# Attention A: the transfers of the relative-position rows split once more, into even and odd rows

## The reference

```python
pos   = (sinusoid_pos_emb(S, D) @ Wp + bp)          # S x 16 per head
content_score = einsum('bhsp,bhtp->bhst', q + u, k)
pos_score     = einsum('bhsp,htp->bhst',  q + v, pos)
pos_score     = _relative_shift(pos_score)
weights = softmax((content_score + pos_score) / sqrt(16))
out     = weights @ val

def _relative_shift(x):                              # b, h, s, s
    x = pad(x, one zero column in front)             # rows of s+1
    x = x.reshape(b, h, s + 1, s)                    # read again as rows of s
    return x[:, :, 1:, :].reshape(b, h, s, s)
```

## Time and profile before

| what | us |
|---|---|
| median of three runs | 11101.68 (11082.91 to 11107.82) |
| the profiled execution, its own time | 11115.23 |
| its span, first to last instruction | 11113.4 |
| busy: TensorE / ScalarE / VectorE / GpSimd | 9422.7 / 6687.5 / 6258.0 / 2944.3 |
| transfers in attention A, writes and reads | 2048 + 2048, 512 KB each |

### The profile page before, as it was taken

The page is one execution under the profiler, slowest core; times in us unless marked ns, Lnnn a source line. Parts: engine busy times, 40 slices in busy tenths (PEclk is TensorE's granted clock), DMA queues, the critical chain, the costliest instruction groups (busy, mean ns, idle before and its releaser), DMA issues. The chain is left out here.

```text
span 11113.4 us, 271423 instructions
## 1 busy us (share of the span) xinstructions
PE 9422.7 (85%) x95520; PEld 6711.5 (60%) x95520; DVE 6258.0 (56%) x14730; ACT 6687.5 (60%) x11009; POOL 2944.3 (26%) x3520
## 2 busy tenths in 40 slices
PE   5888888999688888899968888889996888888999
PEld 3665665666465666566646656656663565665666
DVE  3655663765365566376446556637644565663764
ACT  3666663765466666376546666637644666663764
POOL 2333332001233333200123333310012333331001
PEclk7999999999899999999989999999998999999999
DMA  6999992000699999100069999911007999991100
GB/s 240 378 363 366 381 378 87 26 25 16 233 377 366 361 379 380 59 25 25 16 254 380 367 362 382 365 46 27 23 18 265 373 372 362 379 357 48 27 22 26
DMA packets 747623, 2482.45 MB, mean 223 GB/s; under 512 B 111745, under 2 KB 133761, under 8 KB 745921
## 3 DMA queue, kind: packets, MB, share of 16 engines
q1 hardware_dynamic: 746176, 2463.84, 60.3%
HBM read 1280.34 MB, written 1183.07 MB: 222 GB/s over the span
## 5 line engine op out<-in xcount | busy, mean ns | idle before, releaser
L658 DVE CUSTOM_DVE_ANT_0 z<-sc,z 128x1024 f32<-128x1024 f32 x2048 | 2496.5, 1220 | 1848.5 <-DMA z<-rel_rows 1608.0
L716 POOL TENSOR_SCALAR z<-z,nmax 128x1024 f32<-128x1024 f32 x2048 | 2277.8, 1123 | 4028.5 <-DVE nmax L668 4028.5
L631 ACT ACTIVATE pT<-rg 128x512 f32<-128x512 f32 x4096 | 2445.9, 598 | 738.7 <-PE rg L541 679.5
L541 PE MATMUL rg<-ident,z 128*128 128x128 f32 x16384 | 2527.0, 277 | 77.0 <-issue 68.3
L639 ACT ACTIVATE rel<-rg 128x512 f32<-128x512 f32 x3072 | 1721.1, 596 | 1407.2 <-PE rg L522 1401.8
L541 PEld LDWEIGHTS rg<-ident,z 128*128 128x128 f32 x16384 | 1990.3, 142 | 784.6 <-ACT rel L639 294.4
L522 PE MATMUL rg<-pos_s,qv_s 96*128 96x512 bf16 x4096 | 1590.8, 396 | 1021.4 <-DVE rel L693 901.6
L1013 DVE CUSTOM_DVE_ANT_0 z<-sc,mask 128x1024 f32<-128x1024 f32 (+7 forms) x1536 | 1359.1, 910 | 227.0 <-PE sc L832 173.9
L952 ACT ACTIVATE pT<-rg 128x512 f32<-128x512 f32 (+3 forms) x1792 | 928.4, 550 | 763.0 <-PE rg L885 751.0
L522 PEld LDWEIGHTS rg<-pos_s,qv_s 96*128 96x128 bf16 x4096 | 478.7, 118 | 1498.0 <-DVE rel L693 1150.9
L960 ACT ACTIVATE z<-z,nmax 128x128 f32<-128x128 f32 (+15 forms) x1024 | 1226.6, 1198 | 89.0 <-POOL nmax L978 76.7
(11 more groups left out here) (93 smaller groups left out, 8161.5 us busy)
## 6 DMA issues: line engine op xcount, KB each, us to landing
rel_rows<-rel SPq DMA_DIRECT2D x2048, 512.0 KB, 7.2
z<-rel_rows SPq DMA_DIRECT2D x2048, 512.0 KB, 7.1
xnT<-qu_parts SPq DMA_DIRECT2D x792, 64.0 KB, 2.3
xnT<-v_heads SPq DMA_DIRECT2D x132, 256.0 KB, 4.3
v_heads<-rel SPq DMA_DIRECT2D x8, 4096.0 KB, 12.5
k_sb<-k_parts SPq DMA_DIRECT2D x408, 64.0 KB, 2.3
qv_s<-qv_parts SPq DMA_DIRECT2D x384, 64.0 KB, 6.2
pos_s<-pos_parts SPq DMA_DIRECT2D x384, 64.0 KB, 7.2
```

What stands on the lines that cost most here:

```text
L541: mm = e.transpose(rg[:, T_BANK[q], (j - 4 * q) * P:(j - 4 * q + 1) * P], z[:, n % RING, j * P:(j + 1) * P], ident[:, :])
L631: e.activation(pT[:, t % 2, q * CH:(q + 1) * CH], rg[:, T_BANK[q], :], ACT.Exp, scale=SCALE).then_inc(p_ready[q], 1)
L658: e.tensor_tensor_reduce(out=zs, in0=scf[:, 2 * half * CH:2 * (half + 1) * CH], in1=zs, scale=1.0, scalar=-3.0e38, op0=ALU.add, op1=ALU.ma ...
L716: e.tensor_scalar(zs, zs, 1.0, nmax[:, n % 2:n % 2 + 1], ALU.mult, ALU.add).then_inc(AA[done], 1)
```

## The change

Each column half of a write or a read becomes two transfers of 64 rows x 1024 floats, one of the even and one of the odd rows: 64 partitions in steps of 2 on the SBUF side, a row pitch of two rows in device memory. Within a half the order is read even, write even, read odd, write odd. The write's waits stand ahead of the even write only. The counts of the two semaphores go from 32 to 64 a tile.

```diff
-                                for per in (G, G // OB, 32 * G // RING, HB // NB * QK_INC, HB // NB * 16)))
+                                for per in (G, G // OB, 64 * G // RING, HB // NB * QK_INC, HB // NB * 16)))
...
-            return base.moves + 32 * (n // RING + 1)
+            return base.moves + 64 * (n // RING + 1)
...
-            def read_half(n, half):
+            def read_part(n, half, odd):
...
-                shifted = bass.AP(tensor=rel_d.tensor, offset=hd * FLAT + (i0 + 1) * S + c0, ap=[[S, P], [1, S // 2]])
-                e.dma_start(z[:, k, c0:c0 + S // 2], shifted).then_inc(rel_in[k], 16)
-
-            def write_half(base, n, half):
+                shifted = bass.AP(tensor=rel_d.tensor, offset=hd * FLAT + (i0 + odd + 1) * S + c0,
+                                  ap=[[2 * S, P // 2], [1, S // 2]])
+                e.dma_start(z[odd:P:2, k, c0:c0 + S // 2], shifted).then_inc(rel_in[k], 16)
+
+            def write_part(base, n, half, odd):
...
-                for c in ((R_DVE, R_ACT[-1]) if half else (R_ACT[1],)):
-                    e.wait_ge(r_copied[c], e.snap(base.tiles + (n + 1)))
-                    settle(e)
-                there = bass.AP(tensor=rel_d.tensor, offset=hd * FLAT + i0 * (S + 1) + 1 + c0, ap=[[S + 1, P], [1, S // 2]])
-                e.dma_start(there, rel[:, k, c0:c0 + S // 2]).then_inc(rel_out[k], 16)
+                if not odd:
+                    for c in ((R_DVE, R_ACT[-1]) if half else (R_ACT[1],)):
+                        e.wait_ge(r_copied[c], e.snap(base.tiles + (n + 1)))
+                        settle(e)
+                there = bass.AP(tensor=rel_d.tensor, offset=hd * FLAT + (i0 + odd) * (S + 1) + 1 + c0,
+                                ap=[[2 * (S + 1), P // 2], [1, S // 2]])
+                e.dma_start(there, rel[odd:P:2, k, c0:c0 + S // 2]).then_inc(rel_out[k], 16)
...
                 for half in range(2):
-                    if here(n):
-                        read_half(n, half)
-                    if here(r):
-                        write_half(base, r, half)
+                    for odd in range(2):
+                        if here(n):
+                            read_part(n, half, odd)
+                        if here(r):
+                            write_part(base, r, half, odd)
```

## The result

The changed kernel takes **12165.01 us** (median of 4 runs, 12142.59 to 12186.07) against 11104.75 us before: a ratio of 1.0958, 95% interval 1.0927 to 1.0989. It is slower by 1060 us; I had said 11830, and 11040 to 12500 as the range. The profile after has a span of 12142.9 us, 1029.5 more than before.

The account below looks back on a forecast made before the run. Attention A, 55% of the span, was taken to last as long as its DMA packets take. 11115 us plus 690 for stepped rows and 41 for small packets made 11846, less 14 for the median: some 11830, range 11040 to 12500.

Parts of the forecast that it names:

- What bounds the kernel: Attention A, 55% of the span, lasts as long as its DMA packets take; the queue is always full.
- Bytes, finer alternation: Attention A's transfers: bytes and large packets stay, finer turns between reads and writes save nothing; taken as 0, at best -563 us.
- Small packets: Four more transfers a tile add 64 small packets at 10 ns each, 4 on each engine: 41 us.
- Stepped rows: Attention A's transfers of 64 rows in steps of two have slower packets: +690 us, at most +2072; chance 0.45.
- rival 1: The queue hides all: stepping costs nothing, only small packets are left; 11102 to 11160 us, chance 0.22.
- SP's queue: SP's four more issues a step, 1.3 to 1.9 us, are covered by its 2.1 us of waiting: 0.
- rival 2: SP's issuing bounds the steps with operand loads: +140 us, +422 at most, 11283 us with small packets; chance 0.13.
- Order: The odd read behind the even write and its waits leaves later, but the 7.2 us queue covers it: 0.
- Rival 3: Smaller pieces land sooner and VectorE waits less, rate above 373 GB/s: -110 us, 10990 us; chance 0.20.
- The signs: Expected profile after: attention A's DMA share about 1.0, 333 GB/s, four stretches 6800 us together, VectorE's wait near 2300 us.
- Q: Theory set up for the experiments: SyncE's issuing of transfers is the bound of the changed kernel.
- F: Theory in the experiments, the forecast's own: transfers of 64 stepped rows are slower for the DMA engines.

Follow-up runs that it names:

- e9: Kernel before with 29 satisfied waits on SyncE behind each of a step's four transfers, the transfers unchanged; 12060 us (1.0857).
- e2: Kernel before without the operand loads of heads 2 and up in attention A; 10819 us (0.9735).
- e10: Changed kernel with both reads ahead of both writes in each half; 12248 us (1.1027).
- e3: Changed kernel with its even and odd rows at full width (64 rows x 2048 floats), so four transfers a tile; 11638 us (1.0472).
- e8: Kernel before with each write and each read as one transfer of 128 rows x 2048 floats; 11481 us (1.0327).
- e7: Kernel before with twelve stretches ahead of the first batch: writes, reads and both in turn, each in four transfer forms; 11280.81 us in all.
- e6: Kernel before with twelve satisfied waits on SyncE behind each of a step's four transfers; 11276 us (1.0142).
- e11: Changed kernel with the two writes of the lower half issued by ScalarE instead of SyncE; 11726 us (1.0557).
- e12: Changed kernel with the lower half's writes issued by ScalarE and without the operand loads of heads 2 and up in attention A; 11460 us (1.0317).
- e1: Changed kernel without the operand loads of heads 2 and up in attention A; 11635 us (1.0469).
- e4: Changed kernel with the first 64 and the last 64 rows in place of the even and the odd; 13003 us (1.17).
- e5: Changed kernel with each of a tile's eight transfers taking all 128 rows and a quarter of the columns; 12024 us (1.0814).

## Why the prediction was right and wrong

The direction and the range held; the time was 335 us too low, and its main reason was wrong. That the number came so near is luck: 690 of the 731 us forecast stood for a cost that the runs did not find, and most of the 1060 that came fell, by e9, to a term that I had put at 0.

- **What bounds the kernel.** Right: e2, which takes 5% of the bytes from a full queue, gained. The queue of 7.2 us was full before, and the loss shows in idle DMA engines (99.6 to 91.2% busy) and longer packets (176 to 188 ns).
- **Bytes, finer alternation.** No gain by finer turns was seen, as said. No run here separates a small gain or loss (e10).
- **Small packets.** 41 us. The size was right: summed over the traces' own rows (300 to 1500 us), a small packet takes 9 to 10 ns, before and after, where I took 10. e3 against e8, where their number doubles too, leaves 157 us net for them and for two more issues together.
- **Stepped rows, +690 us.** This step failed. It carried the 236 ns of the 16-row loads over to 64 rows. e7 has 64 stepped rows writing in the same 5.4 us as 128, and at full width reading and in turn as fast; only for the change's own form, in turn, are 6% left open. The loads' 16 rows are another form, and they came alone; rival 1 had said so. The upper bound of 2072 us stood on no row of this stage.
- **SP's queue, 0; rival 2, +140 and +422 at most.** This is where the time went. The mechanism was described as it came, with its sign in the profile (share below 0.97, no waits for ScalarE's copies). What was mis-sized is first the price of an issue: I took it from 128-row transfers, 0.33 alone and 0.43 behind another, when the earlier trace rows also had transfers of fewer rows, at 0.59. The 64-row transfers take 0.45 at least and 0.60 behind another. With that the same sum reads 8 x 0.6 + 2 x 0.56 + 0.9 = 6.8 us in a step with loads, and 5.7 in the others, 6.5 in the mean; the trace has 6.68 and, in the step with the values' load, 6.06. The mean is 6.96, so 0.4 us of it is not in the sum; some issues last over 1 us. The second error: SyncE's 2.1 us of waiting were counted as cover for 1.3 to 1.9 us, when 3.2 us came; and e6 lost 1.4% with 1.1 us of it.
- **Order, 0.** Nothing speaks against it (e10), though e10 has hardly any waits to stand behind.
- **Rival 1** fell on the total, though its premise, that stepping by two costs nothing, held. **Rival 3** fell: in the changed kernel no rate above 373.
- **The signs.** Rate 333 GB/s forecast, 318 measured; four stretches of 6800 us together, 7121; VectorE's wait 2300, 2258; share 1.0, 0.91. VectorE's wait, and the rate nearly, would have looked like a confirmation. Only the share, and SyncE's waits, told the mechanisms apart.

So it is shown that SyncE has no slack after the change and that this alone can cost 948 us; that nothing else in the 64-row form costs anything is not shown. Of the times written down beforehand, Q's came true in e9 and nearly in e10 (12230 at most, 12248 measured), F's in e6, e11 and e12, and neither's in e1, e3 and e4. Open: why e1 and e12, whose SyncE has 11 and 21% of its time to wait, are still 816 and 641 us above e2. A SyncE that spreads one tile's eight issues over 5 us hands the DMA engines less ahead at any time, and time to landing in the stage is 4.7 to 6.3 us in them against 6.5 to 6.7 in e2; that fits, but it is argued, not shown. The rival is that the form itself is slower for the engines: the 6% of e7's middle stretch would be some 350 us of the stage, an estimate (0.06 x 6094 is 366, a little less in e2's shorter stage), so it could be a part of the 816 and hardly all. No run here beats the kernel before with all of its work done.

## What to carry to other kernels

Before splitting transfers, add up the issuing queue as if it were an engine: number of transfers in a step by the price of one in the form they will have, plus waits and gaps, and compare with the step. A queue that issues for a saturated DMA needs slack, since it must stay ahead: here the loss began with half of its waits gone (e6, 1.4%) and was 8.6% with nearly all gone (e9). And when the bound is in doubt, give the suspected queue idle work in the old kernel (e9): it costs one edit and leaves the transfers as they are.

## What the runs showed of the hardware

- An issue on SyncE is not dearer for more rows but for fewer: 314 ns at least for 128 rows (512, 1024 or 2048 wide), 444 to 451 for 64 rows (1024 or 2048 wide; stepped or in a row); behind another, 0.43 and 0.60 us. For 64 rows back to back that is 256 KB in 0.64 us (e7), 410 GB/s at most, hardly above the 373 that the DMA engines moved before.
- The Trainium skill, DMA: Bandwidth & Descriptors, "Issuing engines are not separate DMA queues", calls the sequencer's time for a DMA usually small relative to the DMA itself. Here it was 0.6 us against 0.64 us to move 256 KB at the stage's best rate of 411 GB/s, so at this size the trace disagrees.
- 64 rows in a row move at 250 GB/s where 64 stepped rows of the same width move at 403 and 128 rows (half as wide) at 388 (e7, writing alone). In the kernel e4, eight transfers a tile of this form, is 17% slower than the kernel before, the change 9.6%.
- The small packets, 4 bytes each, one on each engine behind a transfer, take 9 to 10 ns where a 4 KB packet takes 174 in the mean (the trace of before, 300 to 1500 us).
- Halving the packet to 2 KB with full DMA engines took the rate from 373 to 326 GB/s (e5).
- Packets of the same form last longer when the queue is thin (190 ns in e9, 176 before), so a longer mean packet is no proof of a slower form.
